# Feed-forward of a transformer layer: gate and up as seven block products over both batches, then down with its whole weight in SBUF

## Chip, cores and metric

One core of one Trainium2 chip runs the whole program. The metric is the device time in microseconds from start to end of one execution; three executions of the kernel before took 3243.32, 3244.49 and 3246.14 us, a median of 3244.49.

## What is computed

A pre-norm transformer layer in float32, two sequences ("batches") of 1024 tokens, width 1024, 32 heads, feed-forward width F = 2752. Cut to what matters here:

```python
x = x + attention(layernorm(x)) @ attn_ow + attn_ob
t = layernorm(x)                        # 2 x 1024 tokens, 1024 wide
up, gate = t @ W_up.T, silu(t @ W_gate.T)   # 2752 wide
x = x + (gate * up) @ W_down.T          # back to 1024
```

## The kernel before

Every engine has its own instruction stream. `schedule()` writes one list of steps by hand, and each engine walks that list and takes from each step what concerns it; so the order of the list is the order of every engine's queue, SP's (which issues all DMAs) included. An engine waits on a semaphore inside its own stream, and all that stands behind the wait in that stream waits too.

**Precision.** A float32 product is made of three fp32r matmuls (`product3`, L657 to L660): an operand is split into a high part (a Copy to fp32r on ScalarE) and a low part (the operand minus the high part, a subtraction on VectorE), and high*high, low*high and high*low are added in one PSUM bank. One matmul contracts 128 rows and makes 128 x 512 outputs.

**Attention** (to 1710 us) and the **output projection** of batch 1 (`project`, L189) run first. The projection computes, for each of eight token tiles of 128 tokens, two halves of 512 columns with 24 matmuls each, in two PSUM banks that VectorE empties (`osum`, L1097), loads the context with `ctload` (L1319, two DMAs of 512 KB from `n_d` in runs of 128 floats), adds a residual loaded by `xrload` (the bias is added on GpSimd, L1169) and stores the sum to `y_d` in HBM. Between its tiles it loads back (`nload`), normalizes (`nnorm`) and transposes on TensorE (`tr`, L685) the eight tiles of batch 0, and splits them from PSUM into `x2h` (L851) and `x2l` (L1020), 128 x 8 x 1024 each, which fill 64 KB of every partition.

**Feed-forward** (L400 to L455) goes batch by batch. F is cut into 22 blocks of 128 rows, the last of 64 rows; the last 64 rows of up are put beside the last 64 of gate, so a batch has 43 weight tiles. For a block `f`, `gate_up` issues four products (gate and up, two halves of 512 tokens), each of 8 contraction tiles x 3 = 24 matmuls in a bank of its own (L776 to L792). ScalarE makes silu of gate from PSUM (L928), VectorE multiplies with up (L1116), and the two split the hidden block into `hh` and `hl` in SBUF (L939, L1121), where four blocks have room. After every second block `down` (L794 to L816) adds two blocks of the hidden layer into the output: for each of 8 token tiles and 2 halves a group of 6 matmuls in one of four banks, which VectorE adds to `y` in SBUF (L1131, 352 times in all). A pair of blocks of down's weight is loaded into `draw` and split by GpSimd (L1183, L1185) into `dh`, `dl`; gate and up tiles are loaded to `graw` (512 KB each) and split by ScalarE (L918) and VectorE (L1107), one weight tile for 1024 tokens. Between the batches, `x2h` and `x2l` are refilled: 16 groups of four transposes go between down groups of the last two pairs of batch 0.

## Time and profile before

| what | value |
|---|---|
| median of three executions | 3244.49 us |
| the profiled execution, its own time | 3244.88 us |
| its span, first to last instruction | 3243.3 us |
| TensorE matmuls, busy | 14464, 3165.0 us (98% of the span) |
| VectorE, ScalarE, GpSimd busy | 61%, 45%, 24% |
| mean granted TensorE clock | 0.995 |
| HBM read, written | 228.41 MB, 84.41 MB |
| first gate matmul, last down matmul | 1815.48 us, 3238.95 us |

A row of a group of instructions reads: line, engine, operation, tile written <- tiles read, shapes, how many | busy us in all, mean ns of one | idle time of that engine just before them, and who ended it. The duration of a matmul is modelled and overlaps with the next: the distance from start to start is what it costs. A clock of 1.00 is 2.4 GHz, 0.50 is 1.2 GHz.

### The profile page before, as it was taken

The page shows a single profiled execution, that of the slowest core. Times are in us where ns is not written, and L with a number is a line of the kernel's source. Part 1 is how long each engine was busy: PE and PEld are TensorE (multiplying, and loading weights), DVE is VectorE, ACT ScalarE, POOL GpSimd, SP SyncE. Part 2 cuts the span into 40 slices and gives each one's busy share as a digit, 9 for nine tenths or more (in the row PEclk, how much of TensorE's full clock was granted, in tenths as well). Part 3 has the DMA queues.
Part 4 walks back from the last instruction along what each step waited for, and adds up shares of the span by engine and source line. Part 5 has one row for each costly group of instructions (what it writes and reads, how often), then busy time and mean ns, then how long its engine had stood idle before and what let it go on. Part 6 is the DMA issues. An engine that isn't in the chain of part 4 may idle for free.

```text
span 3243.3 us, 38858 instructions
## 1 busy us (share of the span) xinstructions
PE 3165.0 (98%) x14464; PEld 2479.8 (76%) x14464; DVE 1993.9 (61%) x3104; ACT 1456.5 (45%) x2696; POOL 794.2 (24%) x583
## 2 busy tenths in 40 slices
PE   7999999999999999999999999999999999999999
PEld 7766777767777776766677888888888888888887
DVE  6888888998898998989864323322334333233324
ACT  1577787777787787877650211111112111111111
POOL 1234433333344433433332110101011001010110
PEclk9999999999999999999999999999999999999999
DMA  3433343452333333336438411111111411111111
GB/s 118 129 120 114 92 131 95 122 156 76 121 109 105 118 111 102 113 104 199 131 118 267 144 63 52 39 40 63 55 52 59 181 53 39 40 59 59 40 52 52
DMA packets 146028, 315.90 MB, mean 97 GB/s; under 512 B 24944, under 2 KB 58864, under 8 KB 142256
## 3 DMA queue, kind: packets, MB, share of 16 engines
q1 hardware_dynamic: 145840, 313.42, 30.8%
q8 instruction: 114, 1.87, 0.2%
q14 instruction: 74, 0.61, 0.1%
HBM read 228.41 MB, written 84.41 MB: 96 GB/s over the span
## 4 chain that ended last, share of the span: by engine, by line
PE 86%; DVE 10%; ACT 2%; issue 1%; DMA 1%; SPq 1%; POOL 0%; ACTq 0%; DVEq 0%
PE ps L658 16%; PE ps L659 16%; PE ps L660 16%; PE ps L724 6%; PE ps L743 6%; PE ps L755 6%; PE ps L760 6%; PE ps L813 5%; PE ps L814 5%; PE ps L815 5%; DVE mx L1054 3%; DVE pl L1076 3%; DVE wl L1026 1%; ACT ph L884 1%; ACT pu L883 1%
## 5 line engine op out<-in xcount | busy, mean ns | idle before, releaser
L883 ACT ACTIVATE pu<-ps 128x512 f32<-128x512 f32 x1024 | 617.5, 603 | 337.3 <-PE ps L743 334.1
L1054 DVE TENSOR_REDUCE mx<-ps 128x1 f32<-128x512 f32 x1024 | 696.6, 685 | 113.5 <-PE ps L724 102.9
L1154 POOL TENSOR_TENSOR pl<-pu,ph 128x512 fp32r<-128x512 f32 x315 | 429.5, 1363 | 947.1 <-ACT ph L884 946.7
L884 ACT ACTIVATE ph<-ps 128x512 fp32r<-128x512 f32 x1024 | 616.2, 602 | 0.0
L1076 DVE TENSOR_TENSOR pl<-pu,ph 128x512 fp32r<-128x512 f32 x709 | 553.8, 782 | 58.3 <-ACT ph L884 55.2
L658 PE MATMUL ps<-x2h,gh 128*128 128x512 f32 x1376 | 535.6, 389 | 0.8 <-DVE x2l L1020 0.8
L659 PE MATMUL ps<-x2h,gl 128*128 128x512 f32 x1376 | 535.4, 389 | 0.0
L660 PE MATMUL ps<-x2l,gh 128*128 128x512 f32 x1376 | 535.4, 389 | 0.0
L1116 DVE TENSOR_TENSOR hf<-ps,sg 128x512 f32<-128x512 f32 (+1 forms) x88 | 60.9, 692 | 694.7 <-PE ps L660 686.0
L724 PE MATMUL ps<-kst,qst 96*128 96x512 f32 x1024 | 415.0, 405 | 21.3 <-DVE mx L1054 20.1
L743 PE MATMUL ps<-qst,kst 98*128 98x512 f32 x1024 | 409.9, 400 | 5.7 <-ACT ph L884 5.2
L755 PE MATMUL ps<-ph,vt 128*65 128x512 f32 x1024 | 412.2, 403 | 0.8 <-ACT uu L890 0.8
L760 PE MATMUL ps<-pl,vt 128*65 128x512 f32 x1024 | 404.9, 395 | 0.0
L928 ACT ACTIVATE sg<-ps 128x512 f32<-128x512 f32 (+1 forms) x88 | 52.6, 598 | 694.0 <-PE ps L660 694.0
L1183 POOL TENSOR_SCALAR dh<-draw 128x1024 fp32r<-128x1024 f32 x44 | 46.2, 1049 | 1245.0 <-DMA draw<-in_wd 621.9
L1131 DVE TENSOR_TENSOR y<-ps,y 128x512 f32<-128x512 f32 x352 | 236.8, 690 | 161.8 <-PE ps L815 147.9
L658 PEld LDWEIGHTS ps<-x2h,gh 128*128 128x128 f32 x1376 | 258.4, 188 | 54.8 <-issue 1.2
L659 PEld LDWEIGHTS ps<-x2h,gl 128*128 128x128 f32 x1376 | 258.4, 188 | 53.6
L660 PEld LDWEIGHTS ps<-x2l,gh 128*128 128x128 f32 x1376 | 258.4, 188 | 53.4
L813 PE MATMUL ps<-dh,hh 128*128 128x512 f32 x672 | 264.5, 394 | 0.3
L814 PE MATMUL ps<-dh,hl 128*128 128x512 f32 x672 | 261.8, 390 | 0.0
L815 PE MATMUL ps<-dl,hh 128*128 128x512 f32 x672 | 261.7, 389 | 0.0
(91 smaller groups left out, 4515.9 us busy)
## 6 DMA issues: line engine op xcount, KB each, us to landing
wraw<-in_wqkv SPq DMA_DIRECT2D x24, 1024.0 KB, 5.7
qst<-q_d SPq DMA_DIRECT2D x192, 128.0 KB, 2.9
kst<-k_d SPq DMA_DIRECT2D x192, 128.0 KB, 3.0
graw<-in_wg SPq DMA_DIRECT2D x44, 512.0 KB, 4.5
graw<-in_wu SPq DMA_DIRECT2D x42, 512.0 KB, 3.5
draw<-in_wd SPq DMA_DIRECT2D x42, 512.0 KB, 3.9
q_d<-stg SPq DMA_DIRECT2D x64, 256.0 KB, 2.4
k_d<-stg SPq DMA_DIRECT2D x64, 256.0 KB, 2.4
```

The source lines that it names most:

```text
L658: e.matmul(dst, ah, bh, start=(k == 0), stop=False)
L659: e.matmul(dst, al, bh, start=False, stop=False)
L660: return e.matmul(dst, ah, bl, start=False, stop=last)
L724: e.matmul(ps[2 + n][:, :], qst[j % 3][0:96, tile_of(t)], kst[j % 3][0:96, halves(half)], start=True, stop=True).then_inc(s["p_a"], 1)
L743: e.matmul(ps[(n - 1) % 2][:, :], kst[j % 3][:, tile_of(t)], qst[j % 3][:, halves(half)], start=True, stop=True).then_inc(s["p_st"], 1)
L755: e.matmul(bk[0:65, :], vv, ph[sl][:, :], start=(t == 0), stop=False)
L760: e.matmul(bk[0:65, :], vv, pl[sl][:, :], start=False, stop=(t == TT - 1)).then_inc(s["p_pv"], 1)
L883: e.activation(pu[sl][:, :], bk[:, :], ACT.Exp, scale=SCALE).then_inc(s["a_p"], 1)
L884: e.activation(ph[sl][:, :], bk[:, :], ACT.Exp, scale=SCALE).then_inc(s["a_ph"], 1)
L1054: e.reduce_max(mx[:, j % 2, t, half:half + 1], ps[2 + bank_of["a", j, t, half]][:, :], AX.X).then_inc(s["v_mx"], 1)
L1076: e.tensor_tensor(pl[sl][:, :], pu[sl][:, :], ph[sl][:, :], ALU.subtract).then_inc(s["v_pl"], 1)
L1154: e.tensor_tensor(pl[sl][:, :], pu[sl][:, :], ph[sl][:, :], ALU.subtract).then_inc(s["g_pl"], 1)
```

## The change

Only the feed-forward and what prepares it change; attention stays, and the output projection keeps its matmuls.

**Seven products.** The contraction (1024) is cut in two halves of 512, the tokens of a batch in two halves of 512, and the 256 weight rows of a step are gate block f and up block f. From the four sub-blocks of activations seven combinations are formed, from the four of weights seven combinations, and a unit `u` (one f of one batch; 44 units, 22 per batch) is seven products of 4 contraction tiles x 3 = 12 matmuls each, instead of four of 24. The last unit of a batch has half the rows and takes 12 + 24 + 12 matmuls as plain products. The four results are sums of the seven products: product 0 is copied from PSUM by ScalarE to `gx`, and VectorE makes seven sums from PSUM in `gx`, `gu`, `gy`, `gz`. Products use four banks in turn.

**Weights.** One DMA of 1 MB loads gate and up of a unit; GpSimd forms three combinations with four additions of 128 x 512 (`gs`); ScalarE and VectorE split each of the seven 128 x 4 x 128 operands (`gsp`) into a ring of 7 slots, five products ahead.

**Activations.** Token tiles are transposed in pairs i (tiles i and 4 + i), and ScalarE (four copies) and VectorE (four sums) write seven 128 x 4 x 128 combinations to one buffer `eb`, which goes to `b_d` in HBM (`bst`, 1.83 MB in runs of 128 floats, four per batch). Later seven blocks of 1 MB come back (`bload`, two buffers `braw`), and ScalarE and VectorE split each in two steps (`bsp`) into `bh`, `bl`. For batch 0 the pairs follow projection tiles 1 to 4 and the loads start after tile 5. Batch 1's pairs lie inside units 2, 4, 6 and 8, and its blocks are split around the change of batch.

**Hidden and down.** Gate times up is stored to `h_d` in HBM (`hst`, 256 KB, two per unit). Down comes after both batches: all 22 blocks of its weight are loaded (`dload`, two buffers), split by ScalarE and VectorE (`dsp`) and stay in SBUF. Ten are split during the last two units, twelve at the start of down, where room comes free. Then 16 token tiles ("visits") take 130 matmuls each in two banks, with hidden tiles loaded (`hin`) and split (`hsp`) in two chunks of 11 blocks per visit, and one addition of the residual per half at the end (`yadd`).

The core of the diff:

```diff
...
+AHEAD_G = 5
+RING = 7
...
+                elif t <= 4:
+                    until("nnorm", 2, 2 * t - 1)
+                    paired(2, t - 1)
+                    if t < 4:
+                        for m in (2 * t, 2 * t + 1):
+                            defer(1, "nload", 2, m)
+                elif t == 5:
+                    for m in range(2):
+                        step("bload", 0, m)
+                    step("gin", 0)
+                    step("gs", 0)
+                    defer(6, "bsp", 0, 0)
+                    defer(7, "bload", 0, 2)
+                    defer(9, "gsp", 0, 0)
+                    defer(11, "bsp", 0, 1)
+                    defer(12, "bload", 0, 3)
+                elif t == 6:
+                    defer(1, "gsp", 0, 1)
+                    defer(3, "bsp", 0, 2)
+                    defer(4, "bload", 0, 4)
+                    defer(6, "gsp", 0, 2)
+                    defer(8, "gsp", 0, 3)
+                    defer(9, "gin", 1)
...
+    for m in range(3, 7):
+        then(0, m - 3, *[("bsp", 0, m)] + [("bload", 0, m + 2)] * (m < 5))
...
+    for i in range(4):
+        then(2 + 2 * i, 0, ("nnorm", 3, 2 * i), ("nnorm", 3, 2 * i + 1))
+        then(2 + 2 * i, 3, ("pair", i))
+        if i < 3:
+            then(2 + 2 * i, 5, ("nload", 3, 2 * i + 2), ("nload", 3, 2 * i + 3))
+    then(NU - 2, 0, ("bload", 1, 0), ("bload", 1, 1))
+    for m, at_ in enumerate([(NU - 1, 4), (NU - 1, 5), (NU - 1, 6), (NU, 0), (NU, 1), (NF, 0), (NF, 1)]):
+        then(*at_, *[("bsp", 1, m)] + [("bload", 1, m + 2)] * (m < 5))
+    late = B * NF
+    for m in range(2):
+        then(late - 5, 2 * m, ("hin", m))
+        then(late - 4, 2 * m, ("hsp", m))
+    then(late - 3, 0, ("dload", 0), ("dload", 1))
+    for f, at_ in enumerate([(late - 2, 2), (late - 2, 3), (late - 2, 4), (late - 2, 5), (late - 2, 6), (late - 1, 0),
+                             (late - 1, 0), (late - 1, 1), (late - 1, 1), (late - 1, 1)]):
+        then(*at_, ("dsp", f), ("dload", f + 2))
+    early = 10
...
+    for i, (u, q) in enumerate(order):
+        want = needs[min(i + AHEAD_G, len(order) - 1)]
+        for v in (want[0] - 1, want[0]):
+            for r in range(operands(v) if v >= 0 else 0):
+                if (v, r) <= want and (v, r) not in split:
+                    if r == 0 and v:
+                        step("gs", v)
+                    split.add((v, r))
+                    step("gsp", v, r)
+                    if r == operands(v) - 1 and v + 2 < hidden:
+                        step("gin", v + 2)
+        step("g", u, q)
+        for s in ready:
+            step("mul", *s)
+            step("hst", *s)
+        ready = []
+        last = products(u) - 1
+        for half, r in ((0, last - 1), (1, last)) if u % NF < NU else ((1, 1), (0, 2)):
+            if q == r:
+                step("silu", u, half)
+                ready.append((u, half))
...
+            for f in range(early, NF):
+                step("dsp", f)
+                if f + 2 < NF:
+                    step("dload", f + 2)
+                if f == 12:
+                    step("hin", 2)
+                if f == 15:
+                    step("hsp", 2)
+                    step("hin", 3)
+            step("yin", 0)
...
+        bh = [at(f"bh{q}", kb, [P, 4, 512], f32r, start) for q, (kb, start) in enumerate(bq)]
+        bl = [at(f"bl{q}", kb + 8, [P, 4, 512], f32r, start) for q, (kb, start) in enumerate(bq)]
+        braw = [at(f"braw{i}", 120 + 8 * i, [P, 4, 512]) for i in range(2)]
+        graw = [at(f"graw{i}", 16 + 8 * i, [P, 2, KT, P]) for i in range(2)]
...
+        dh = [at(f"dh{f}", kb, [P, H], f32r, start) for f, (kb, start) in enumerate(dq)] + [at("dh21", 131, [P, H], f32r)]
...
+                        terms = [[(0, 0)], [(0, 3), (1, 6)], [(1, 5)]][q]
+                    for i, (w, x_) in enumerate(terms):
+                        r = of_operand(u, w)
+                        pe.wait_ge("v_gl", r)
+                        pe.wait_ge("v_bl", of_block_of(b, x_))
+                        sl = (r - 1) % RING
+                        for k in range(4):
+                            m = product3(bk[:, :], gh[sl][:, k, :], gl[sl][:, k, :], bh[x_][:, k, :], bl[x_][:, k, :], 4 * i + k,
+                                         4 * i + k == 4 * len(terms) - 1)
...
+                    def down(f, half):
+                        i, z = f % CH, halves(half)
+                        h_, l_ = hh[f // CH][:, i, :], hl[f // CH][:, i, :]
+                        pe.wait_ge("v_hl", 2 * v + f // CH + 1)
+                        pe.wait_ge("v_dl", f + 1)
+                        e.matmul(banks[half][:, :], h_, dh[f][:, z], start=(f == 0), stop=False)
+                        if f < NF - 1:
+                            e.matmul(banks[half][:, :], l_, dh[f][:, z], start=False, stop=False)
+                        return e.matmul(banks[half][:, :], h_, dl[f][:, z], start=False, stop=(f == NF - 1))
+
+                    if v < B * TT - 1:
+                        for f in range(CH * c, CH * c + CH):
+                            for half in range(2):
+                                m = down(f, half)
...
+                    q, n = PLACE[b][m], 7 * b + m
+                    act.wait_ge(f"d_b{n % 2}", 16 * (n // 2 + 1))
+                    if b:
+                        act.wait_ge("p_g", block_free(b, q))
+                    elif q >= 3:
+                        act.wait_ge("p_o", of_o(B * TT - 1, 1))
+                    for i in range(2):
+                        z = slice(2 * i, 2 * i + 2)
+                        e.activation(bh[q][:, z, :], braw[n % 2][:, z, :], ACT.Copy).then_inc(s["a_bh"], 1)
...
+                    act.wait_ge("p_g", ring_free(n))
+                    if n < RING:
+                        act.wait_ge("p_o", of_o(B * TT - (3, 1)[n > 4], 1))
+                    e.activation(gh[n % RING][:, :, :], gu_operand(u, q), ACT.Copy).then_inc(s["a_gh"], 1)
...
+                    act.wait_ge(f"d_d{draw_of(f)}", 16 * draws(f))
+                    act.wait_ge("p_g", down_free(f))
+                    if f >= 14:
+                        act.wait_ge("v_h", of_hidden(B * NF - 1, 1))
+                    if f == NF - 1:
+                        act.wait_ge("v_dl", NF - 2)
...
+                    elif q == 3:
+                        dve.wait_ge("d_hs1", 16 * u)
+                        dve.wait_ge("v_po", of_sum(u, 1))
+                        e.tensor_tensor(gz[:, :], bk[:, :], gy[:, :], ALU.add).then_inc(s["v_po"], 1)
+                        e.tensor_tensor(gu[:, :], bk[:, :], gu[:, :], ALU.add).then_inc(s["v_po"], 1)
+                    elif q == 4:
+                        dve.wait_ge("v_po", of_sum(u, 2))
+                        e.scalar_tensor_tensor(gy[:, :], bk[:, :], -1.0, gy[:, :], ALU.mult, ALU.add).then_inc(s["v_po"], 1)
...
+                        e.tensor_tensor(s0, a21, a22, ALU.add).then_inc(s["g_s"], 1)
+                        pool.wait_ge("g_s", of_weights(u, 0))
+                        e.tensor_tensor(a21, a11, a21, ALU.subtract).then_inc(s["g_s"], 1)
+                        e.tensor_tensor(s1, s0, a11, ALU.subtract).then_inc(s["g_s"], 1)
+                        pool.wait_ge("g_s", of_weights(u, 2))
+                        pool.wait_ge("v_gl", of_operand(u, 1))
+                        e.tensor_tensor(s1, a12, s1, ALU.subtract).then_inc(s["g_s"], 1)
...
+                    copy(b_d[n - 2, :, :, :, tile_of(i)], eb[:, :, :, :], "d_bs")
+
+                elif what == "bload":
+                    b, m = at_
+                    n = 7 * b + m
+                    sp.wait_ge("d_bs", 16 * 4 * (b + 1))
+                    if n >= 2:
+                        sp.wait_ge("v_bl", of_block(0, n - 2))
...
+                    if f >= 2:
+                        sp.wait_ge("v_dl", f - 1 if f < NF - 1 else f)
...
+                    if c == 0:
+                        copy(hraw[c][:, :, :], h_d[b, 0:CH * P, q].rearrange("(k p) s -> p k s", p=P), f"d_h{c}")
...
```

## Rows read from the trace of the kernel before

**Rows 1.** The page's parts 1 and 2: busy time, span in 40 slices

```profile
PE 3165.0 (98%) x14464; PEld 2479.8 (76%) x14464; DVE 1993.9 (61%) x3104; ACT 1456.5 (45%) x2696; POOL 794.2 (24%) x583
...
DVE  6888888998898998989864323322334333233324
```

**Rows 2.** Table by stretch of time, the projection to the end

```profile
core 0: us, PE busy (x) PEld busy (x) DVE busy (x) ACT busy (x) POOL busy (x), PEclk, DMA share, GB/s
...
1710.00:1815.00 105.00, 102.80 (x472) 85.36 (x472) 45.21 (x76) 11.94 (x21) 19.15 (x8) 0.97 0.70 220
...
1886.00:2480.00 594.00, 593.84 (x2608) 488.77 (x2608) 191.75 (x255) 79.40 (x110) 65.42 (x38) 1.00 0.15 50
2480.00:2530.00 50.00, 47.94 (x240) 38.91 (x239) 33.07 (x51) 10.41 (x19) 6.92 (x4) 1.00 0.41 145
```

**Rows 3.** Timeline of PE, one run of gate and up, then one of down

```profile
2099.86 0.39 PE L658 MATMUL ps<-x2h,gh 128*128 128x512 f32 x1
...
2143.38 0.39 PE L813 MATMUL ps<-dh,hh 128*128 128x512 f32 x1
...
2165.45 0.39 PE L658 MATMUL ps<-x2h,gh 128*128 128x512 f32 x1
```

**Rows 4.** Timeline of PE: before the feed-forward, its first and last matmul

```profile
1812.78 1.91 PE L685 MATMUL ps<-idt,turn 128*128 128x128 f32 x16
1815.48 0.47 PE L658 MATMUL ps<-x2h,gh 128*128 128x512 f32 x1 [0.79 <-DVE x2l L1020]
...
3238.95 0.39 PE L810 MATMUL ps<-dl,hh 128*128 128x512 f32 x1
```

**Rows 5.** The chain that ended last: start of a down run, transposes between the batches

```profile
2083.37 0.50 PE ps L813
2083.87 0.24 PE ps L814
...
2482.45 0.87 PE ps L685 x8
```

**Rows 6.** Instructions by tile: ns min/median/max; or by group: mean ns

```profile
L1107 DVE TENSOR_TENSOR gl<-graw,gh x86: 1211/1224/2305, 1791.9 to 3170.4; 128x1024 fp32r<-128x1024 f32 x86
...
L1121 DVE TENSOR_TENSOR hl<-hf,hh x84: 692/692/2754, 1828.1 to 3190.1; 128x512 fp32r<-128x512 f32 x84
...
L1131 DVE TENSOR_TENSOR y<-ps,y x352: 674/692/692, 1885.7 to 3239.4; 128x512 f32<-128x512 f32 x176
...
L1154 POOL TENSOR_TENSOR pl<-pu,ph x315: 1266/1292/1850, 113.6 to 1659.5; 128x512 fp32r<-128x512 f32 x158
...
L918 ACT ACTIVATE gh<-graw 128x1024 fp32r<-128x1024 f32 x86 | 86.2, 1046 | 16.4 <-DMA graw<-in_wg 9.9 <-PE ps L810 4.0 <-DMA graw<-in_wu 2.5
...
L939 ACT ACTIVATE hh<-hf 128x512 fp32r<-128x512 f32 x84 | 53.1, 632 | 435.4 <-DVE hf L1116 435.4
```

**Rows 7.** The page's part 6, whole run: KB each, median us to landing

```profile
wraw<-in_wqkv SPq DMA_DIRECT2D x24, 1024.0 KB, 5.7
...
q_d<-stg SPq DMA_DIRECT2D x64, 256.0 KB, 2.4
```

**Rows 8.** Timeline, 1841 to 1847 us: GpSimd, then VectorE

```profile
1841.36 2.41 POOL L1185 TENSOR_TENSOR dl<-draw,dh 128x1024 fp32r<-128x1024 f32 x1
...
1842.55 3.44 DVE L1107 TENSOR_TENSOR gl<-graw,gh 128x1024 fp32r<-128x1024 f32 x2 [2.87 <-ACT gh L918]
```

**Rows 9.** DMAs, 1740 to 1800 us: all packets; context loads with median to landing

```profile
DMA packets 12494, 14.03 MB, mean 234 GB/s; under 512 B 433, under 2 KB 10311, under 8 KB 12491
...
ct<-n_d SPq DMA_DIRECT2D x8, 512.0 KB, 6.0
```

**Rows 10.** Timeline of PE around the one long wait in the projection

```profile
1711.89 0.80 PE L658 MATMUL ps<-xh,ct 128*128 128x512 f32 x1 [5.13 <-DVE xr L1102]
...
1717.96 0.39 PE L660 MATMUL ps<-xl,ct 128*128 128x512 f32 x1
```

**Rows 11.** Loads of down's weight by tile: us to landing, min/median/max

```profile
DMA to landing us min/median/max: 3.4/3.9/9.9
```

More of the change, by code:

```diff
@@ L23 @@
 POOL_PL = (1, 4, 7, 10, 13)
[L24 removed]
+NU = NF - 1
+CH = NF // 2
+AHEAD_G = 5
+RING = 7
 NW = 3 * NG
[L26 removed]
 FIRST = [(0,), (1,), (2, 3), (4, 5), (6, 7)]
[L28 removed]
+PLACE = [(0, 1, 2, 3, 4, 5, 6), (1, 2, 4, 0, 3, 6, 5)]
 def schedule():
@@ L77, in schedule, with paired @@
     follow["osum"] = lambda n, half: [(1, ("ostat", n)), (1, ("ystore", n))] if half else []
+    def paired(n, i):
+        for m in (2 * i, 2 * i + 1):
+            for g in range(2):
+                step("tr", n, m, g)
+        step("e", n, i)
+        step("bst", n, i)
     def transposed(n, t):
@@ L630, in internal @@
+        dl = [at(f"dl{f}", kb + 4, [P, H], f32r, start) for f, (kb, start) in enumerate(dq)] + [at("dl21", 149, [P, H], f32r)]
+        yb = [at(f"yb{i}", (153, 70)[i], [P, 512]) for i in range(2)]
         def internal(name, shape):
@@ L1387, in program @@
+            for half in range(2):
+                sp.wait_ge(f"d_out{half}", 16 * TT * B)
         bank_of = {}
```

638 lines of the change are left out of this document (366 added, 272 removed).

## Prediction, on record before the changed kernel ran

> **What bounds the kernel.** I read the page's busy times and slices first, to see which engine has no idle time; then the table by stretch, to see whether that holds in the part that changes; then TensorE's timeline, for the price of one matmul, since modelled durations overlap; then the groups and DMA tables for the price of everything the change adds. TensorE is busy 98% of the span, while VectorE falls from 8 tenths of a slice to 2 to 4 in the feed-forward, the right half of the row [rows 1]. In the long stretch from 1886 to 2480 us TensorE is busy 593.84 of 594 us at full clock, with DMA at 0.15 of its capacity and VectorE at 192 us of 594 [rows 2]: the feed-forward is bound by the number of matmuls, and every other resource has two thirds free there. The projection ahead of it is another place: DMA's share is 0.70 over 105 us [rows 2].
>
> The price of a matmul: the run of gate and up from 2099.86 to 2143.38 has 192 matmuls in 43.52 us, 0.2267 us each. The down run behind it has 96 in 22.07 us, 0.2299 [rows 3]. The whole feed-forward runs from 1815.48 to 3238.95, 1423.5 us [rows 4]. Its 4128 + 2080 = 6208 matmuls at 0.2267 are 1407.4 us; the 64 transposes among them, eight groups of eight at 0.87 [rows 5], are 7.0; so 9.1 us are waits, in the down runs and at the change of batch, where 50 us hold only 240 matmuls [rows 2].
>
> **What goes away.** A unit takes 7 x 12 = 84 matmuls in place of 4 x 24 = 96; 42 full units save 504. The two last units stay at 48, and down stays at 2080. 504 x 0.2267 = **-114.3 us** [rows 3]. Down's groups of six with a bank change and an addition each become runs of 65 in a bank: the first matmul of a down run has 0.50 us on the chain where others have 0.24 [rows 5], and the run's mean is 0.0032 us above the gate's, 2080 x 0.0032 = 6.7 us; with the waits around the change of batch, whose refilling of x2h and x2l moves into units with free engines, I take **-8 us** (between 0 and -9.1). The transposes stay in number. The last ones ahead of the first gate matmul and the wait for their split take 1815.48 - 1812.78 = 2.7 us [rows 4], of which the transposes (0.8) move elsewhere: **-2 us**. 320 of the 352 VectorE additions to y, all work of GpSimd on down's weight and half the loads of down's weight go too, and cost nothing now because TensorE covers them.
>
> **What a unit costs the other engines.** A unit is 84 x 0.2267 = 19.0 us of TensorE. VectorE: seven sums from PSUM at 0.69, two multiplications and seven low parts at 0.69 [rows 6], 16 x 0.69 = 11.0 us. ScalarE: seven high parts, one copy, two silu, 10 x 0.63 = 6.3. GpSimd: four additions at 1.29 = 5.2 [rows 6]. DMA: 1 MB in, 0.5 MB out, 83 GB/s. None reaches 19.0, and the normalizing, transposing and pairing of batch 1 (8 x 0.69 on VectorE per pair) fits into what is left of units 1 to 9, as do the moved `rstd` and reloads. Each product has four banks and the ring of operands is five products (13.6 us) ahead, so TensorE waits only if VectorE is more than three products (8.2 us) late; the stores that hold gy and gz have 7 us, and such a store lands in 2.4 [rows 7]. I cost this at 0; if the cover went, each of 294 products could pay a bank change like that of the down run, 0.50 - 0.24 = 0.26 us, 76 us at most. Gate and up change banks every 24 matmuls in [rows 3] and show no such gap, which is nearer to what is added, so 0.
>
> VectorE's subtraction of two SBUF tiles takes 692 ns as a rule, but 2754 at worst [rows 6]. The timeline shows why: GpSimd's L1185 runs from 1841.36 to 1843.77, and two L1107 that begin at 1842.55 take 3.44 us in place of 2.45 [rows 8]; the first was held until GpSimd had ended. In a unit nine VectorE operations have two SBUF inputs (7 + 2) and GpSimd has 5.2 us, so VectorE can lose 5.2 us at most: 11.0 + 5.2 = 16.2, still under 19.0, and I take the loss for TensorE as 0. The Trainium skill (SBUF — State Buffer, "SBUF: two separate sides") states this as a rule: VectorE with two SBUF inputs and a GpSimd operation that reads SBUF hold a shared port pair for a whole instruction each. It speaks against the change, and the third rival is what it could come to.
>
> **The projection and the first unit.** Per tile the projection moves 1 MB of context (2048 runs of 512 bytes), 0.5 MB each of residual, store and reload: 14.03 MB in 60 us, 234 GB/s, and a context load takes 6.0 us to land [rows 9]. The change adds in tiles 1 to 4 a second reload and 1.83 MB of `bst` in the same short runs per tile, so about 5.0 MB per 12.7 us, 390 GB/s, two thirds more than is seen. eb is single: the next pair's copies wait for the store, which has some 9 us. By the context's rate (1 MB in 6.0) it needs 11 us. I take 1 us of stall for each of three pairs, **+3** (0 to 10). Behind it, in SP's order, block loads wait for the last `bst` and then hold `gin`: about 9 us after the pair's sums the 2 MB of the first blocks start and land 6 to 8 us later (1 MB takes 5.7 [rows 7]), some 12 us ahead of the projection's end; their splits (ScalarE 2 x 1.05, VectorE 2 x 1.22 [rows 6]) and the operand split stand in VectorE's queue before the `osum` that frees TensorE's bank, and GpSimd's `gs` before the last bias addition. TensorE waits about **+4** there (0 to 12). In unit 0, blocks 3 to 6 can be split only once the projection is done, and each block takes load 5.7 + 1.05 + 2 x 1.22 with two buffers, while products come every 2.7 us and VectorE has 1.3 us of its own work per product. Stepping through it, block 5 is ready at about 16 us where product 5 wants it at 13.6, and block 6 two more late: **+4.5** (2 to 12). A wait of 5.13 us made the clock fall: matmuls from 1711.89 to 1717.96 stand 0.43 us apart, 14 in 6.07 us instead of 3.17, 2.9 us lost [rows 10]. One such fall here: **+2.5** (0 to 2.9). Together +14, between +2 and +37.
>
> **Change of batch**: the blocks of batch 1 are split while the last unit's 24-matmul product runs; I find each ready in time and take **+1** (0 to 6).
>
> **Down's weight.** This is the largest new wait. One dload/dsp round of a buffer is: landing 3.9 us [rows 11], ScalarE 1.05, VectorE 1.22 [rows 6], 0.1 for semaphores, 6.3 us for two buffers, so one block per 3.15 us; TensorE uses a block in 6 x 0.2267 = 1.36. Count from the start of unit 42: down starts at 19.0 + 48 x 0.2267 = 29.9. The first `dsp` stands behind product 2's sum in VectorE's queue and is done at 3 x 2.72 + 0.69 + 1.22 = 10.1, the second behind product 3's two sums at 4 x 2.72 + 1.38 + 1.22 = 13.5; ten rounds later blocks 20 and 21 are ready at 73 and 76.5, with the split of hidden chunk 2 among them. The first visit ends one block later, at about 77.5, and not at 29.9 + 29.5 = 59.4: **+18**. During it TensorE works less than half the time, so I expect the clock at 1.2 GHz and one recovery as in [rows 10]: **+3**. With landing at 3.4 [rows 11] and no fall it is +13; with the splits also waiting on each other, +28.
>
> [...]
>
> After the first visit nothing waits: a visit is 29.5 us, its two chunks of 0.72 MB load in short runs (about 4.3 us each by [rows 9]) and split in 1.4 + 1.7 us each, half a visit ahead. The end is the same one addition and store.
>
> **Sum**, against the profiled execution's 3244.9: -114.3 - 8 - 2 + 14 + 1 + 21 = -88.3, **3156.6**; that execution stands 0.4 above the median, so 3156 us.
>
> **Rivals.** (1) *The starts are covered better*: loads land at their minimum and the clock does not fall, new waits 15 instead of 36: 3135 us. For it: DMA is nearly idle at down's start, a share of 0.15 in the stretch before [rows 2]. Against: the round of two buffers is serial by its waits. (2) *DMA saturates in the projection, or product changes cost something*: 23 us more in the projection and unit 0 (its upper bound), or 0.1 us at each of 294 products, 29 us: 3180 to 3210. For it: the share of 0.70 already; against: context loads are asked for a tile and a half early. (3) *VectorE becomes the bound of a unit, slower than before*: if each of the nine two-SBUF operations is held for one GpSimd addition, 11.0 + 9 x 1.29 = 22.6 us per unit against 19.0, 42 x 3.6 = 151 us more: 3307 us. It decides from 19.0 + 88/42 = 21.1 us per unit. Against it: GpSimd has only four additions per unit, which can hold VectorE 5.2 us at most, 16.2 in all. The Trainium skill's page named above (SBUF — State Buffer) has the hold but not how often it falls. (4) *The change doesn't cut the work*: the loops fix 84 matmuls per unit, so only a pitch that grows with twelve-matmul products could do it; 3245.
>
> **Chances.** Forecast, 3140 to 3176: 0.66. Rival 1: 0.12. Rival 2: 0.16. Rival 3: 0.05. Rival 4: 0.01. A measurement of this kernel tells 0.2% (6.5 us) from no change. Faster 0.94, same 0.01, slower 0.05. The range for 8 in 10 takes the forecast, most of rival 1 and the nearer half of rival 2: 3130 to 3192.
>
> **What would show it.** Right: TensorE 13960 matmuls; units 19.0 us apart at full clock; VectorE near 11 to 13 us per unit; one wait of 3 to 5 us near the projection's end and a few us in unit 0; a first visit of some 45 us with TensorE half idle on VectorE's `dl` and the clock at 1.2 GHz, then 29.5 us per visit. Wrong: units longer than 19.5 us, waits of TensorE on PSUM sums in the steady part, or a first visit under 35 us or over 60.

## The result, and the profile of the kernel after

Four executions of the changed kernel took 3188.55 to 3195.46 us, a median of **3192.54 us**, beside 3245.16 us for the kernel before: ratio 0.9838 [0.9821, 0.9855]. The gain is 52.6 us where 89 were forecast, and the median lies half a microsecond above the upper end of the range, less than the 6.9 us between its own fastest and slowest execution; the account below goes by the terms of the sum and not by that half microsecond. The profiled execution took 3192.58 us, its span is 3190.8, and the mean granted clock fell from 0.995 to 0.986.

The page's parts 1 and 2 of the changed kernel answer to [rows 1].

```profile
PE 3070.2 (96%) x13960; PEld 2402.7 (75%) x13960; DVE 2148.2 (67%) x3304; ACT 1617.1 (51%) x2976; POOL 878.0 (28%) x663
...
DVE  6889888898898898988884476655755565211111
```

The work was cut as forecast, 14464 - 13960 = 504 matmuls, and VectorE is busier in the gate and up part (5 to 7 tenths in place of 2 to 4) and idle in down. The table by stretch, with the columns of [rows 2]:

```profile
1714.00:1829.00 115.00, 98.09 (x424) 81.09 (x424) 43.29 (x73) 13.47 (x23) 18.57 (x9) 0.90 0.93 284
...
2022.00:2260.00 238.00, 238.00 (x1055) 197.18 (x1053) 140.88 (x203) 75.89 (x130) 62.72 (x47) 1.00 0.28 102
...
2290.00:2690.00 400.00, 399.85 (x1765) 330.77 (x1764) 241.96 (x342) 128.28 (x215) 106.75 (x77) 1.00 0.26 93
2690.00:2747.00 57.00, 37.58 (x131) 26.67 (x130) 24.52 (x23) 19.05 (x20) 0.00 (x0) 0.85 0.56 177
2747.00:3187.00 440.00, 440.00 (x1942) 364.28 (x1941) 66.90 (x72) 44.33 (x56) 0.00 (x0) 1.00 0.28 82
```

Three long stretches, 1078 us together, have no idle time at full clock. From 2290 to 2690 one matmul costs 400 / 1765 = 0.2266 us, the price of before, in products of twelve matmuls with a change of bank after each. In down it is 440 / 1942 = 0.2266 too, where [rows 3] had 0.2299. What went wrong lies in short stretches: the projection (1714 to 1829, DMA share 0.93, clock 0.90), the first unit, the change of batch, and the first visit of down (2690 to 2747). The table of waits of TensorE from 1714 to 3187 us names them (engine and line that waits, the line waited for; us in total, times, longest):

```profile
PE ps L949 <- DVE dl L1362: 19.4, 11, 4.0
PE ps L821 <- DVE turn L1188: 11.1, 3, 4.3
PE ps L788 <- DVE xr L1278: 10.7, 2, 6.2
PE ps L788 <- DVE bl L1301: 10.2, 4, 4.2
```

The first row is down waiting for its weight, the second the transposes of batch 0's pairs waiting for normalized tiles, the third the projection's bank (4.51 us of it is the one wait that the kernel before has too [rows 10]; the other, 6.17, is new), the fourth the products waiting for a block of the activations. TensorE's timeline gives the ends of the stages: resumption after the old wait, first gate matmul, first down matmul, last matmul.

```profile
1714.26 0.80 PE L788 MATMUL ps<-xh,ct 128*128 128x512 f32 x1 [4.51 <-DVE xr L1278]
...
1842.10 0.39 PE L788 MATMUL ps<-bh,gh 128*128 128x512 f32 x1
...
2687.94 0.39 PE L949 MATMUL ps<-dh,hh 128*128 128x512 f32 x1
...
3187.18 0.39 PE L952 MATMUL ps<-dl,hh 128*128 128x512 f32 x1
```

From these and from the starts of the matmuls between them comes the table on which the rest rests. "Excess" is the time of a stage minus its matmuls at 0.2267 us. The stages are counted from TensorE's resumption, because that moment differs from kernel to kernel, 1708.3 to 1714.8 us in the eight traces of a changed kernel, though nothing ahead of it differs.

| kernel | median us | ratio to before | resumption to first gate matmul | units 0 and 1, excess | around the change of batch, excess | first visit of down |
|---|---|---|---|---|---|---|
| before | 3245.16 | 1 | 103.6 | | | |
| forecast | 3156 | | 111.1 | 4.5 | 1 | 50.6 |
| after | 3192.54 | 0.9838 [0.9821, 0.9855] | 127.8 | 10.1 | 7.2 | 55.5 |
| reload first | 3181.73 | 0.9806 [0.9789, 0.9822] | 117.7 | 10.6 | 7.2 | 54.1 |
| long runs | 3183.17 | 0.9805 [0.979, 0.982] | 120.9 | 9.6 | 7.1 | 54.7 |
| weights early | 3186.44 | 0.982 [0.9805, 0.9834] | 125.2 | 10.5 | 7.2 | 55.0 |
| last block | 3186.46 | 0.9818 [0.9803, 0.9833] | 128.5 | 9.5 | 7.2 | 50.8 |
| no GpSimd sums | 3184.2 | 0.9808 [0.9791, 0.9824] | 129.0 | 3.9 | 7.8 | 54.6 |
| all orders | 3158.75 | 0.9727 [0.9713, 0.9742] | 106.4 | 5.3 | 6.3 | 50.0 |
| three buffers | 3147.04 | 0.9688 [0.9673, 0.9702] | 108.7 | 4.6 | 9.0 | 36.8 |

(The ratio is to the kernel before on the same chip. Its median was 3245.16 us beside the changed kernel, 3245.74 beside reload first, long runs, weights early and last block, and 3247.89 beside no GpSimd sums, all orders and three buffers. The stages come from one trace each. The forecast's 111.1 is 103.6 - 2 + 3 + 4 + 2.5, its 50.6 is 47.6 + 3.) Against the forecast the changed kernel misses 127.8 - 111.1 = 16.7 us in the projection, 5.6 in units 0 and 1, 6.2 around the change of batch, 4.9 in the first visit, and 2.4 because TensorE resumed at 1714.26 and not at 1711.89: 35.8 of the 36.0 us between 3156.6 and 3192.58.

**The projection.** SP's timeline shows what stands between one pair and the next (start, duration of the issue, DMA):

```profile
1749.30 0.62 SPq L1448 DMA_DIRECT2D b_d<-eb  x1
1749.98 5.81 SPq L1448 DMA_DIRECT2D turn<-y_d  x2
1755.83 0.56 SPq L1448 DMA_DIRECT2D y_d<-xr  x1
1756.43 3.13 SPq L1448 DMA_DIRECT2D ct<-n_d  x2
```

The reload of the next two tiles (512 KB each) stands behind the store of `eb`, and the issue of these two DMAs alone took 5.81 us, 4.52 of it the first. VectorE normalizes the first of them only at 1760.39, after 9.00 us of waiting, and TensorE starts its transposes at 1761.35:

```profile
1760.39 0.81 DVE L1188 TENSOR_SCALAR turn<-turn,mv,rq 128x1024 f32<-128x1024 f32 x1 [9.00 <-DMA turn<-y_d]
```

The DMAs of the same window as [rows 9], with the median time to landing, show the crowd: a context load lands in 9.2 us in place of 6.0.

```profile
DMA packets 19332, 15.46 MB, mean 258 GB/s; under 512 B 353, under 2 KB 17735, under 8 KB 19330
...
b_d<-eb SPq DMA_DIRECT2D x3, 1792.0 KB, 9.0
turn<-y_d SPq DMA_DIRECT2D x6, 512.0 KB, 8.9
ct<-n_d SPq DMA_DIRECT2D x6, 512.0 KB, 9.2
```

The new wait for the bank is an order in VectorE's own stream. The timeline of all engines before 1829.71:

```profile
1823.23 2.36 DVE L1301 TENSOR_TENSOR bl<-braw,bh 128x1024 fp32r<-128x1024 f32 x2 [8.27 <-ACT bh L1061]
...
1827.77 1.20 DVE L1307 TENSOR_TENSOR gl<-graw,gh 128x512 fp32r<-128x512 f32 x1 [2.18 <-ACT gh L1072]
...
1828.89 0.68 DVE L1278 TENSOR_TENSOR xr<-ps,xr 128x512 f32<-128x512 f32 x1
...
1829.71 0.77 PE L788 MATMUL ps<-xh,ct 128*128 128x512 f32 x1 [6.17 <-DVE xr L1278]
```

VectorE waits 8.27 us for a block that is late, then 2.18 for a weight (`gin` stands in SP's queue behind two block loads), and only then empties the bank (L1278) for which TensorE has stood since its matmul of 1823.16.

**The change of batch.** VectorE's timeline there:

```profile
2264.95 4.21 DVE L1301 TENSOR_TENSOR bl<-braw,bh 128x1024 fp32r<-128x1024 f32 x2 [0.26 <-ACT bh L1061]
2269.09 1.77 DVE L1307 TENSOR_TENSOR gl<-graw,gh 128x512 fp32r<-128x512 f32 x1
2270.79 0.68 DVE L1354 TENSOR_TENSOR gz<-gz,gu 128x512 f32<-128x512 f32 x1
2271.39 2.35 DVE L1301 TENSOR_TENSOR bl<-braw,bh 128x1024 fp32r<-128x1024 f32 x2
```

GpSimd's timeline in the same microseconds, the additions for unit 23's weight:

```profile
2264.10 1.75 POOL L1435 TENSOR_TENSOR gs<-graw 128x512 f32<-128x512 f32 x1
2265.93 2.16 POOL L1437 TENSOR_TENSOR graw<-graw 128x512 f32<-128x512 f32 x1
2268.04 2.28 POOL L1438 TENSOR_TENSOR gs<-gs,graw 128x512 f32<-128x512 f32 x1
```

While GpSimd adds, VectorE's split takes 4.21 us in place of 2.35 and the operand split 1.77 in place of 0.68. TensorE stands from 2269.82 to 2273.89 for the split that ends at 2273.74, and the next twelve matmuls come at half clock. The 7.2 us of this stage are that one wait, 3.8 us over the usual distance, and 3.3 behind it, most of them the half clock.

**Down's start.** Counted from the start of unit 42 (2658.04), the first split of down's weight ended at 10.2 us, the second at 13.5, down's first matmul came at 29.9 and block 20 at 76.6, where the prediction had 10.1, 13.5, 29.9 and 73. Block 21 came at 83.5 in place of 76.5. The landing of the loads of down's weight, as in [rows 11]:

```profile
DMA to landing us min/median/max: 3.4/3.5/5.5
```

ScalarE's timeline, its splits of blocks 20 and 21:

```profile
2732.30 1.06 ACT L1103 ACTIVATE dh<-draw 128x1024 fp32r<-128x1024 f32 x1 [2.46 <-DMA draw<-in_wd]
2739.24 1.06 ACT L1103 ACTIVATE dh<-draw 128x1024 fp32r<-128x1024 f32 x1 [5.89 <-DMA draw<-in_wd]
```

VectorE's split of block 21:

```profile
2740.33 1.23 DVE L1362 TENSOR_TENSOR dl<-draw,dh 128x1024 fp32r<-128x1024 f32 x1 [5.72 <-ACT dh L1103]
```

And TensorE, which waits for it:

```profile
2741.61 0.79 PE L949 MATMUL ps<-dh,hh 128*128 128x512 f32 x1 [4.02 <-DVE dl L1362]
```

The last block follows 6.94 us behind block 20, where the others are 2.2 to 4.5 apart, 3.3 on average: its load goes to `draw0`, which block 20 holds (`draw_of` gives 0 for both), so it starts only when block 20 is split.

### The profile page after: what moved, and what is told of

It is laid out like the page before. It is cut to its first block and busy times, and to the rows that moved or that the text cites. A ratio compares the mean times of both kernels' runs of the same rounds, so it can differ in the third digit from the quotient of the medians.

```text
span 3190.8 us, 38696 instructions
## 1 busy us (share of the span) xinstructions
PE 3070.2 (96%) x13960; PEld 2402.7 (75%) x13960; DVE 2148.2 (67%) x3304; ACT 1617.1 (51%) x2976; POOL 878.0 (28%) x663
## 5 line engine op out<-in xcount | busy, mean ns | idle before, releaser
L788 PE MATMUL ps<-bh,gh 128*128 128x512 f32 x1208 | 473.4, 392 | 10.2 <-DVE bl L1301 10.2
L789 PE MATMUL ps<-bh,gl 128*128 128x512 f32 x1208 | 472.3, 391 | 0.0
L790 PE MATMUL ps<-bl,gh 128*128 128x512 f32 x1208 | 472.1, 391 | 0.0
L788 PEld LDWEIGHTS ps<-bh,gh 128*128 128x128 f32 x1208 | 228.1, 189 | 59.0 <-issue 11.8
L790 PEld LDWEIGHTS ps<-bl,gh 128*128 128x128 f32 x1208 | 228.3, 189 | 47.8
L789 PEld LDWEIGHTS ps<-bh,gl 128*128 128x128 f32 x1208 | 228.3, 189 | 47.4
L860 PEld LDWEIGHTS ps<-kst,qst 96*128 96x128 f32 x1024 | 196.0, 191 | 77.9 <-DVE mx L1230 45.4
L879 PEld LDWEIGHTS ps<-qst,kst 98*128 98x128 f32 x1024 | 193.7, 189 | 58.9 <-ACT ph L1019 14.3
L896 PEld LDWEIGHTS ps<-pl,vt 128*65 128x65 f32 x1024 | 141.9, 139 | 93.4 <-issue 1.4
L1441 POOL TENSOR_TENSOR gs<-graw,gs 128x512 f32<-128x512 f32 x42 | 54.4, 1295 | 549.8 <-DVE gl L1307 549.8
```

Source lines behind the costliest of these rows:

```text
L788: e.matmul(dst, ah, bh, start=(k == 0), stop=False)
L789: e.matmul(dst, al, bh, start=False, stop=False)
L790: return e.matmul(dst, ah, bl, start=False, stop=last)
L860: e.matmul(ps[2 + n][:, :], qst[j % 3][0:96, tile_of(t)], kst[j % 3][0:96, halves(half)], start=True, stop=True).then_inc(s["p_a"], 1)
L879: e.matmul(ps[(n - 1) % 2][:, :], kst[j % 3][:, tile_of(t)], qst[j % 3][:, halves(half)], start=True, stop=True).then_inc(s["p_st"], 1)
L896: e.matmul(bk[0:65, :], vv, pl[sl][:, :], start=False, stop=(t == TT - 1)).then_inc(s["p_pv"], 1)
```

## The experiments

For the projection one theory (A) was that the order in the queues makes TensorE wait; the rival (B) that the bytes do, whatever their order: the share of DMA is 0.93 of the stretch, near rival 2 of the prediction. For units 0 and 1 and the change of batch the theory was VectorE held by GpSimd, the rival the order and the two buffers of the blocks. For down's start: the two buffers, and the last block's extra round.

**Reload first.** The reload of the next pair is issued ahead of `eb`'s store.

```diff
                 step("tr", n, m, g)
+        if i < 3:
+            for m in (2 * i + 2, 2 * i + 3):
+                step("nload", n, m)
+                defer(7, "nnorm", n, m)
         step("e", n, i)
...
-                    if t < 4:
-                        for m in (2 * t, 2 * t + 1):
-                            defer(1, "nload", 2, m)
```

> One change to the changed kernel: the reloads of the next pair of token tiles (two of 512 KB) are issued ahead of the store of the seven combinations (1.83 MB in runs of 128 floats), not behind it. Theory A, order in SP's queue: the three waits of TensorE for the normalized tiles in the projection (4.25, 3.86 and 3.01 us) go away, the reloads land within 5 us of the pair's transposes instead of some 11, and the whole is 10 to 13 us shorter than 3192.5. Theory B, the DMA engines are full there (share 0.93): the bytes are the same, so the wait moves to the context loads or to eb's store, and the gain is under 4 us. GpSimd and the later stages stay as they are.

Measured: the projection took 117.7 us in place of 127.8, and the transposes no longer wait at all. The table of waits of this kernel:

```profile
PE ps L950 <- DVE dl L1363: 16.8, 10, 5.1
PE ps L789 <- DVE xr L1279: 16.0, 4, 10.1
PE ps L789 <- DVE bl L1302: 12.9, 5, 5.1
```

No row of L822 waiting for `turn` is left. Its projection in the table by stretch:

```profile
1713.00:1829.00 116.00, 103.09 (x466) 84.61 (x467) 56.47 (x83) 17.09 (x28) 26.48 (x12) 0.94 0.94 299
```

Over the whole stage, from the resumption to the first gate matmul, the same bytes (35 MB) moved in a shorter time, at 298 GB/s in place of 272, so (A) holds for these three waits. The median fell by 10.8 us, as (A) had it. The three waits (11.1 us) are gone, and so is the half clock of the transposes after them (16 took 3.2 us there, 1.67 here, 4.6 us in all). But the wait for the bank grew from 6.17 to 10.11, and two others of 1.29 and 0.93 us appeared at it: 6.2 us were given back, because the blocks on which VectorE's queue hangs came no earlier by as much.

**Long runs.** `eb` is stored so that a row of it is one run of 2 KB, and the matmuls read the block in another order of its columns.

```diff
-                            m = product3(bk[:, :], gh[sl][:, k, :], gl[sl][:, k, :], bh[x_][:, k, :], bl[x_][:, k, :], 4 * i + k,
+                            m = product3(bk[:, :], gh[sl][:, k, :], gl[sl][:, k, :], bh[x_][:, :, tile_of(k)], bl[x_][:, :, tile_of(k)], 4 * i + k,
...
-                    copy(b_d[n - 2, :, :, :, tile_of(i)], eb[:, :, :, :], "d_bs")
+                    copy(b_d[n - 2, :, :, i, :], eb[:, :, :, :].rearrange("p q k c -> p q (k c)"), "d_bs")
```

> One change to the changed kernel: the activation blocks lie pair by pair, so that a pair's combinations are stored in runs of 2 KB instead of 512 bytes, same bytes, same order. If short runs are what fills the DMA engines: a store of 1.83 MB lands in 5 to 6.5 us instead of 9.0, the three waits of TensorE for normalized tiles shrink by about 3 us each, and the whole is 7 to 11 us shorter. If the place in the queue alone counts, with the bytes moved at the same rate: the store still takes 8 to 9 us and the gain is under 2. The matmuls read their moving operand in four pieces of 128; if that costs anything, the pitch of 0.2267 us in gate and up would grow.

Measured: 120.9 us in the projection, and a median 9.4 us lower, in the range of the first theory. The mechanism is not the one expected: the store lands in 7.9 us in place of 9.0 (medians), where 5 to 6.5 were expected, and the three waits shrink by 1.0 to 1.6 us each, not 3; the wait for the bank shrinks by 1.6. The DMAs from 1740 to 1800 us:

```profile
DMA packets 11724, 17.25 MB, mean 287 GB/s; under 512 B 353, under 2 KB 6497, under 8 KB 11721
...
b_d<-eb SPq DMA_DIRECT2D x4, 1792.0 KB, 7.9
```

What changed more than the landing is the issue of what stands behind the store. SP's timeline of this kernel at its second store:

```profile
1759.10 0.55 SPq L1448 DMA_DIRECT2D b_d<-eb  x1
1759.70 2.33 SPq L1448 DMA_DIRECT2D turn<-y_d  x2
```

The two reloads take 2.33 us to issue, for 5.81. In the five traces with the store in short runs the DMA right behind it took 4.4 to 7.5 us to issue, in the three with runs of 2 KB 0.6 to 1.0. That is so in batch 1's pairs too, inside units 2, 4 and 6, where the first reload behind the store took 4.52, 4.55 and 4.44 us in the changed kernel and 0.65 or 0.66 in this one, and where TensorE waits for nothing. So the short runs cost in two ways, at the issue and at the landing, and outside the crowded projection too. (B) has a part all the same: with the order as it was, fewer packets for the same bytes give back 6.9 of the 24.2 us. The matmul that reads its moving tile in four pieces of 128 columns keeps its price; units 2 to 14 have the same excess, 7.1 us, all of it transposes.

**Weights early.** The first `gin` is issued a tile and more ahead of the block loads.

```diff
                 elif t <= 4:
+                    if t == 4:
+                        step("gin", 0)
...
                         step("bload", 0, m)
-                    step("gin", 0)
                     step("gs", 0)
```

> One change to the changed kernel: the load of the first unit's weights (1 MB) is issued before the transposes after projection tile 4, not behind the first two block loads after tile 5. Theory: the wait of 6.17 us of TensorE on the projection's bank comes from the operand split standing ahead of that bank's addition in VectorE's queue and waiting for these weights; it falls to about 3 us, which the block loads explain, and the whole is 3 us shorter. Rival: the wait comes from the block loads or from full DMA engines alone; then it stays between 5.5 and 6.5 us and the 1 MB makes the waits before it longer.

Measured: the wait for the bank fell from 6.17 to 2.53 us, as expected (it was 5.71 in last block, whose projection is that of the changed kernel), and the projection from 127.8 to 125.2. Of the 6.1 us by which the median fell, the trace shows these 2.6; in it TensorE also resumed 3.8 us earlier, which the edit cannot have done. The weight was the last link of that wait; the late block remains.

**No GpSimd sums.** The four additions of a unit on GpSimd are left out, and plain quarters of the weight stand in for the combinations; all loads, splits and matmuls stay.

```diff
-            return (raw[:, 0, 0:4, :], s1[:, :, :], raw[:, 1, 0:4, :], s0[:, :, :], raw[:, 1, 4:8, :], raw[:, 0, 4:8, :], s1[:, :, :])[q]
+            return (raw[:, 0, 0:4, :], raw[:, 0, 4:8, :], raw[:, 1, 0:4, :], raw[:, 1, 4:8, :], raw[:, 1, 4:8, :], raw[:, 0, 4:8, :], raw[:, 0, 4:8, :])[q]
...
-                        e.tensor_tensor(s0, a21, a22, ALU.add).then_inc(s["g_s"], 1)
-                        pool.wait_ge("g_s", of_weights(u, 0))
-                        e.tensor_tensor(a21, a11, a21, ALU.subtract).then_inc(s["g_s"], 1)
-                        e.tensor_tensor(s1, s0, a11, ALU.subtract).then_inc(s["g_s"], 1)
-                        pool.wait_ge("g_s", of_weights(u, 2))
                         pool.wait_ge("v_gl", of_operand(u, 1))
-                        e.tensor_tensor(s1, a12, s1, ALU.subtract).then_inc(s["g_s"], 1)
```

> GpSimd's four additions of weight quarters per unit are left out (the operands are plain quarters instead, so the products are not the reference's); all else of the changed kernel stays. Theory: TensorE waits at the change of batch (4.07 us from start to start) because VectorE's splits of activation blocks are held by GpSimd: pairs of splits took 4.21 us in place of 2.35 there, and up to 3.9 and 4.5 in the projection. Without the additions no split of 128 x 1024 takes over 1.3 us, the wait at the change of batch falls to under 1.5 us, the excess of the first two units (10.1 us) to about 6, the steady units stay at 19.04 us, and the whole is 5 to 10 us shorter than 3192.5. Rival: the holds cost nothing that TensorE sees, and these waits come from the loads of the blocks; then both stay within 1 us.

Measured: the excess of units 0 and 1 fell from 10.1 to 3.9, further than the expected 6; 3.0 us of the fall are shorter waits, 3.2 the half clock that no longer follows them. The edit also takes away ScalarE's waits for the sums (two lines not shown), but in the changed kernel's trace ScalarE waited for none of them between 1842 and 1870 us, so the hold is what is left. At the change of batch the excess stayed (7.8 for 7.2), as the rival had it, though the first wait fell as the theory had it: the wait for batch 1's first block in use, 4.07 us from start to start, became 1.1, and a wait of 3.88 for the last of its blocks took its place. ScalarE's timeline:

```profile
2264.70 0.63 ACT L1091 ACTIVATE gz<-gu 64x512 f32<-64x512 f32 x1 [3.65 <-DMA h_d<-gz]
2265.35 2.01 ACT L1061 ACTIVATE bh<-braw 128x1024 fp32r<-128x1024 f32 x2
...
2272.88 0.60 ACT L1080 ACTIVATE gx<-ps 128x512 f32<-128x512 f32 x1 [1.54 <-DVE gy L1352]
2273.37 2.00 ACT L1061 ACTIVATE bh<-braw 128x1024 fp32r<-128x1024 f32 x2
...
2275.79 1.99 ACT L1061 ACTIVATE bh<-braw 128x1024 fp32r<-128x1024 f32 x2
```

ScalarE's silu waits 3.65 us for a store of the hidden block, and the fifth block's split stands behind it. That block landed only at 2263.91, so at most 1.4 us of this wait are passed on. The rest is an order of steps that no run changed: VectorE's sum for the last unit's silu stands behind that split; the copy of unit 22's product 0 (L1080) waits for the multiplication that follows this silu, because both use `gx`; the splits of the last two blocks (2273.37 and 2275.79) stand behind that copy, though the sixth block had landed at 2268.84. From the end of the fourth block's split on VectorE to the matmul that needs the last block, this takes 17.0 us in each of the seven other traces of a changed kernel and 18.2 here. So the hold is the cause of the first wait, and without it this chain makes another; that is read from the traces and from the kernel's waits, and no run took the chain apart.

**Last block.** The parity of down's two buffers is swapped, so that block 21's buffer is free one block earlier.

```diff
         def draw_of(f):
-            return f % 2 if f < NF - 1 else 0
+            return (f + 1) % 2 if f < NF - 1 else 0
...
-                        sp.wait_ge("v_dl", f - 1 if f < NF - 1 else f)
-                    elif f:
+                        sp.wait_ge("v_dl", f - 1)
+                    elif f == 0:
...
```

> One change to the changed kernel: the two buffers for down's weight are swapped, so that the load of the last, half-sized block need not wait for the split of the block before it. Theory: this block cost one more serial round, so it is ready 1 to 2.5 us after block 20 instead of 6.9, the last wait of TensorE at down's start (4.02 us) falls to under 1 us, and the whole is 4 to 6 us shorter. Rival: its double load takes as long in any case, and the gain is under 1 us.

Measured: the first visit fell from 55.5 to 50.8 us, in the expected range. The last block is ready 3.6 us after block 20 in place of 6.9, where 1 to 2.5 were expected, and the last wait fell from 4.02 to 1.94 us, not under 1.

**All orders.** The edits of reload first, long runs, weights early and last block together; the steps of the projection's last tiles are put off so that VectorE empties the bank ahead of the block splits, block 3 is split ahead of product 0, and batch 1's first splits stand one or two products earlier.

```diff
-                    step("gs", 0)
-                    defer(6, "bsp", 0, 0)
-                    defer(7, "bload", 0, 2)
-                    defer(9, "gsp", 0, 0)
-                    defer(11, "bsp", 0, 1)
-                    defer(12, "bload", 0, 3)
+                    defer(5, "gs", 0)
+                    defer(11, "bsp", 0, 0)
+                    defer(12, "bload", 0, 2)
+                    defer(13, "gsp", 0, 0)
+                    defer(19, "bsp", 0, 1)
+                    defer(20, "bload", 0, 3)
...
-    for m, at_ in enumerate([(NU - 1, 4), (NU - 1, 5), (NU - 1, 6), (NU, 0), (NU, 1), (NF, 0), (NF, 1)]):
+    for m, at_ in enumerate([(NU - 1, 2), (NU - 1, 3), (NU - 1, 5), (NU, 0), (NU, 1), (NF, 0), (NF, 1)]):
```

> Same work as the changed kernel, same bytes; steps in another order: reloads ahead of the pair's store, that store in runs of 2 KB, the first weights loaded early, the additions that free the projection's banks ahead of the block splits in VectorE's queue, block 3's split ahead of the wait for product 0 in ScalarE's queue, batch 1's first splits one or two products earlier, and the last block of down's weight not behind the one before it. If order in the queues is the cause of the waits, they add up: the projection from its resumption to the first gate matmul takes 104 to 110 us instead of 127.8, the first two units have 4 to 7 us of excess instead of 10.1, the change of batch 1 to 4 instead of 7.2, the first visit 51 instead of 55.5: 3150 to 3165 us. If the DMA engines are what is full, the projection stays above 114 us and the whole above 3170.

Measured: 3158.75 us, in the range of the first theory. The projection takes 106.4 us, 2.8 more than before the change:

```profile
1713.90:1820.30 106.40, 102.55 (x472) 84.31 (x473) 52.34 (x81) 16.62 (x27) 25.84 (x12) 0.98 0.97 317
```

The DMA engines are busy 0.97 of it, at 317 GB/s, and TensorE waits less than 4 us in it. The bytes that looked like saturation fit, nearly all of them (33.8 MB in the stage for 34.8, as some loads of blocks and weights now come after it). This kernel has both the new order and the long runs; no run had all the orders with short runs, so how much of the 21.4 us each gives is known only from the runs that had one of them. The change of batch was expected at 1 to 4 us and stayed at 6.3.

**Three buffers.** All orders, and a third buffer for down's weight.

```diff
-        draw = [at("draw0", 145, [P, H]), at("draw1", 131, [P, H])]
+        draw = [at("draw0", 145, [P, H]), at("draw1", 131, [P, H]), at("draw2", 140, [P, H])]
...
-            return (f + 1) % 2 if f < NF - 1 else 0
+            return {18: 0, 19: 2, 20: 1, 21: 0}.get(f, f % 3)
...
-        then(*at_, ("dsp", f), ("dload", f + 2))
+        then(*at_, ("dsp", f), ("dload", f + 3))
```

> The kernel with the other orders and a third 512 KB buffer for down's weight while it is loaded and split. Theory: the first visit's wait is the serial round of two buffers (load 3.5, ScalarE 1.06, VectorE 1.23, about 6 us for two blocks); with three, a block comes every 2 us, which starts early enough that TensorE finds each: the first visit takes 30 to 36 us instead of 50.8 to 55.5 and the clock stays up, the whole is 14 to 20 us under the kernel with the other orders. Rival: ScalarE, VectorE or the DMA engines bound the rate, or the splits stand behind the last units' sums; then the gain is under 6 us.

Measured: 3147.04 us, ratio 0.9688 [0.9673, 0.9702], 11.7 us under all orders, where 14 to 20 were expected and under 6 by the rival. The first visit takes 36.8 us in place of 50.0, just over the expected 30 to 36, although the loads land later (7.3 us at worst, median 4.3, for 5.6 and 3.6 in all orders) and the share of DMA rises to 0.79 in that stretch:

```profile
2660.00:2700.00 40.00, 35.47 (x146) 27.91 (x145) 22.32 (x21) 18.23 (x18) 0.00 (x0) 0.96 0.79 251
```

The serial round of a buffer was the bound, as the prediction had it. The projection is 108.7 for 106.4 and the change of batch 9.0 for 6.3, and nothing there differs between the two kernels, so one trace can move a stage by 2 to 3 us. At the change of batch the 2.7 us are TensorE's clock alone: the blocks' splits end at the same times in both, 0.12 us apart. In all orders eight matmuls at half clock fell ahead of the wait for the last block, and the wait took them up (it was 1.32 us). In three buffers that wait was 2.98 us, and twelve matmuls at half clock came behind it, where nothing takes them up. A third buffer for the blocks was not tried.

## Why the prediction went wrong, by its own steps

- **What goes away** (-114.3, -8, -2): the first two right. 504 matmuls went, at an unchanged 0.2267 us. The first gate matmul to the last of down took 3187.18 - 1842.10 = 1345.1 us for 1423.5 [rows 4]; with 5704 matmuls (1293.1), transposes (7.1) and the excesses of the table (10.1, 7.2 and 55.5 - 29.5 = 26.0) only 1.6 us are left, so down's old waits (9.1) are gone nearly whole. The -2 was a misreading of [rows 4]: of the 2.7 us ahead of the first gate matmul 1.91 are the 16 transposes and only 0.79 the wait for their split. All 64 transposes are still done ahead of the first gate matmul, so 0.8 us could go and not 2.
- **What a unit costs the other engines** (0): right. VectorE is busy 241.96 us in 400, which is 21.0 units, 11.5 per unit (forecast 11 to 13), units stand 19.04 us apart, and TensorE waited for no sum. Rival 3 and the second half of rival 2 (a price at each product) fall with this. The hold by GpSimd is there, as the Trainium skill (SBUF — State Buffer, "SBUF: two separate sides") has it, and free in the steady part. There one operand split per unit takes 1.50 us in place of 0.69, a loss of 0.8 us where the prediction bounded it at 5.2. The prediction bounded it for steady units only and never took it into the starts, where it costs 6.2 us (no GpSimd sums).
- **The projection and the first unit** (+14, bounds 2 to 37): this is the step that failed. It measured 127.8 - 103.6 + 0.8 + 10.1 = 35.1, near the far bound, as every term of it came out large together. "I take 1 us of stall for each of three pairs" was 4.25, 3.86 and 3.01, and after each the transposes ran at half clock. I had asked how long `eb` would be occupied by its store, and not what stands behind that store in SP's queue: the reload of the next pair, whose issue alone is held up 5.81 us. For the bank the term +4 was 6.17. Here the mechanism was in the prediction, `gin` behind the block loads and both splits ahead of `osum`, and the size was off: the blocks landed 6.9 and 8.9 us and the weight 10.9 us after their issue, where it had 6 to 8. The +4.5 of units 0 and 1 was 10.1, 6.2 of it the hold. Rival 2 was nearest to what happened (its first half, 23 us more in the projection and unit 0, is what came, and its interval holds the measured median), though its reason was only partly right: DMA's share did reach 0.93, yet with nearly the same bytes in another order and in longer runs the stage needs 106.4 us.
- **Change of batch** (+1, bounds 0 to 6): mis-sized, 7.2, above its bound. "I find each ready in time" left out the hold, the chain from the last unit's silu over product 0's copy to the last two splits, and the half clock behind a wait. The hold is shown for the first wait; the chain is read from the traces, and no run changed it.
- **Down's weight** (+18 and +3): mechanism right, size short. The times from the start of unit 42 agree to 0.1 us for the first splits; ten rounds later block 20 is 3.6 us late, 6.65 us a round in place of 6.3, although a load landed in 3.5 us at the median and not in 3.9; what fills the rest of a round no run took apart. The step missed that block 21 shares block 20's buffer, 4.7 us by the experiment. The clock was not at 1.2 GHz throughout: its mean is 0.85 from 2690 to 2747 us. (The prediction's list of signs has "some 45 us" for a visit that its sum puts at 50.6.)
- **The clock**: one fall was priced in the projection and one in down. After TensorE's resumption 65 matmuls stand 0.43 us apart, 12 in the kernel before: 53 x 0.2 = 10.6 us, and the terms had 5.5. Behind the waits of 3.68 to 6.17 us TensorE ran at half clock each time, as it did behind the wait of 5.13 [rows 10], and behind the shorter ones now and then: behind 2.11 us yes, behind 2.46, 2.63 and 2.85 in down's start no. So a new wait often costs more than its length. No run took the clock alone; the nearest to it is the pair of traces under "Three buffers".

## To carry over

A kernel with one hand-written order of steps turns each moved DMA into a wait for whatever stands behind it in the queue: list, for each large store or load that is added, the next entries of that queue and who waits for them, before asking about bandwidth. Where a stage begins or changes, count the serial rounds of its buffers to the very last block, and price there also what is free in the steady part (engines holding each other, a lowered clock); 33 of the 36 us missed here lay in some 270 us of starts and changes, and none in the 1078 us of steady work. A DMA share of 0.93 is no proof that bytes are the bound: in another order and in longer runs nearly the same bytes took 21 us less.

## What the runs showed of the hardware

- The issue of the next DMA on SP is held up behind a large store in short runs. Behind 1.83 MB in runs of 512 bytes the next DMA took 4.4 to 7.5 us to issue, in five traces; behind the same bytes in runs of 2 KB it took 0.6 to 1.0 us, in three traces. It was 4.44 to 4.55 us also in batch 1's pairs, away from the crowded projection (changed kernel).
- The same 1.83 MB landed in 9.0 us in runs of 512 bytes and in 7.9 in runs of 2 KB (medians from 1740 to 1800 us, changed kernel and long runs); in batch 1's pairs it was 8.7 to 9.3 and 7.8 to 8.5.
- VectorE's pair of splits took 2.35 us alone and 3.40 to 4.51 beside GpSimd's additions; these took up to 2.28 us in place of 1.28.
- Half clock can come after short idle times of TensorE too: behind a wait of 2.11 us that ended at 1855.25, seven matmuls from 1856.8 stand 0.43 us apart. Behind a wait of 2.63 us that ended at 2708.06 none do. It costs nothing where a later wait takes it up: 2.7 us lie between two traces of the same steps, with eight matmuls at half clock ahead of a wait in one and twelve behind it in the other.
